# Source-number halves kept as 32-bit numbers in the attention loop's edge count

## The chip, the cores and the metric

The kernel is one program on one core of a Trainium2 chip. The metric is the time of one execution on the device, in microseconds (us); lower is better. Three runs before the change gave 5123.76 to 5125.2 us, median 5124.44 us.

## The reference, cut to what matters

A graph with 6250 nodes of 256 features and 200000 edges (`src`, `dst`, sorted by `dst`) goes through two blocks of graph layer and expert layer. The first graph layer is an attention over the edges:

```
h = einsum(layernorm(x), W)                # 8 heads of 32
e = leaky_relu(a_src[src] + a_dst[dst], 0.2)
e_exp = exp(e - segment_max(e, dst)[dst])
alpha = e_exp / (segment_sum(e_exp, dst)[dst] + 1e-16)
out = segment_sum(h[src] * alpha, dst)
```

The second graph layer scales each edge by the inverse roots of the two degrees of its ends, so it needs how often each node occurs in `src` and in `dst`:

```
in_deg  = segment_sum(w, src)
out_deg = segment_sum(w, dst)
```

The change lies in the counting of `src`.

## The kernel before

**Edge lists.** `edge_lists` reads the edges as 128 rows by 1792 numbers and splits each source number s into `hi` = s >> 7 (0 to 48) and `lo` = s - 128 hi (0 to 127). Both are written as bf16 tiles by the Vector engine (L691, L692) and stored by the SyncE queue in the DRAM tensor `source_halves` (L674; the places behind the last edge are filled from `src_void`, L670, L671).

**The attention loop.** `gat_edges` walks over 104 batches ("slots") of 16 tiles of 128 edges. A loop body holds four slots (RING = 4), so buffers rotate over four. Five engines work on different batches at one time, in an order written out by hand and kept by semaphores. In the slot in which the chain of batch k runs:

- GpSimd (POOL) issues 16 indirect DMAs a batch (L1262), each fetching 128 rows of 265 numbers by the source numbers in `gat_sources`. It runs up to three batches ahead.
- ScalarE (ACT) waits until all 16 gathers of batch k have landed, and packs their source terms (L1274).
- TensorE (PE) turns these terms (L1493), and sums earlier batches into PSUM (`scatter`, L1520), eight matrix products at a time between the small steps of the chain (L1497, L1504, L1506, L1510).
- The Vector engine (DVE) does, in this order: `count_onehots` of batch k-1 (L1344, two operations, `lo` then `hi`), then from the turned terms on the chain of batch k (L1353 to L1400), mixed with the messages (L1407) of batch k-1 and the adds of finished sums (L1430, L1429). The next slot begins with its `count_onehots`.

`count_onehots` waits for the batch's halves (`cl`) and for the products that read its outputs last (`sc`), writes two one-hots and signals `co`. The queue SP waits for `co` before it loads the halves of a later batch (L1231) and what stands behind that in its order: source numbers (L1235), flags (L1240, L1242), the transpose of the target one-hots (L1221), targets (L1246). TensorE multiplies the two one-hots (L1525) for the count, in step 3 of that batch, long after.

Of the kernel before, what the change touches and what calls it, by code (L numbers as in the profile page):

```python
# [13 lines left out]
BF16 = mybir.dt.bfloat16  # L14
# [5 lines left out]
P = 128  # L20
EPS = 1e-5
NEG_BIG = -1.0e38
CH = 16
# [7 lines left out]
BLK = 256  # L31
# [556 lines left out]
def edge_lists(k, S, ins, T, pj):  # L588

    nc = k.nc  # L590
    BG = S.BG
# [8 lines left out]
    with ExitStack() as ctx:  # L600
# [6 lines left out]
        df = k.sb(ctx, "dst_float", [P, BG, BLK])  # L607
        fs = k.sb(ctx, "starts_flag", [P, BG, BLK])
        fe = k.sb(ctx, "ends_flag", [P, BG, BLK])
        hi = k.sb(ctx, "src_hi", [P, BG * BLK], BF16)  # L610
        lo = k.sb(ctx, "src_lo", [P, BG * BLK], BF16)
        bulk, wrap = full * BLK, BLK // SPREAD
        assert bulk % CH == 0 and wrap % CH == 0 and (rest + 1) * SPREAD < P and bulk + wrap < S.BATCH * CH
        void = k.sb(ctx, "src_void", [P, 2, S.BATCH * CH - bulk], BF16)
        vd = k.sem("src_void_written")
        block = ctx.enter_context(nc.Block())
        src, dst = ins["src"], ins["dst"]
# [484 lines left out]
def gat_edges(k, S, C, T, acc):  # L1102
# [8 lines left out]
    RING = 4  # L1111
# [39 lines left out]
    with ExitStack() as ctx:  # L1151
# [23 lines left out]
        z = k.sb(ctx, "gat_sums", [P, 2 * TH + H])  # L1175
        q = k.sb(ctx, "gat_exponents", [P, TH + H])
        f = k.sb(ctx, "gat_factors", [1, 2, H])
        hl = k.sb(ctx, "count_halves", [P, RING, 2, CH], BF16)
        iob = k.sb(ctx, "count_iota", [P, P, 2], BF16)
        ohl = k.sb(ctx, "count_onehot_lo", [P, CH // 2, P, 2], BF16)  # L1180
        ohh = k.sb(ctx, "count_onehot_hi", [P, CH // 2, NT, 2], BF16)
# [1619 lines left out]
def gnn_moe_kernel(nc, ins, out):  # L2801
    S = Shapes(ins["x"], ins["src"], ins["L0_gnn_W"], ins["L0_ffn_W1"], ins["L1_ffn_w1"])
    NT, D, H = S.NT, S.D, S.H
    with ExitStack() as top:
        k = Core(nc, top)
        C, T = Namespace(), Namespace()
# [33 lines left out]
        T.flags = k.dram("gat_tile_flags", [S.SG * P * SUB, 2 * P])  # L2840
        T.least = k.dram("gat_tile_least", [2, S.SG * P * SUB])
        T.window = k.dram("gat_step_windows", [S.SG * P], I32)
        T.halves = k.dram("source_halves", [P, 2, S.BATCH * CH], BF16)
        T.steps = k.dram("unit_steps", [(S.SUPER + 1) * P, 2])
        T.codes = k.dram("unit_codes", [S.SUPER, P, 2 * P], BF16)
        T.xn = k.dram("normal_rows", [S.ROWS, D])
# [6 lines left out]
        with ExitStack() as gat:  # L2853
            C.adst = k.sb(gat, "a_dst_pieces", [P, NT, 3 * H], BF16)
            C.sources = k.sb(gat, "step_sources", [P, S.SG, P, SUB], I32)
            with ExitStack() as ctx:
                pj = Projection(k, S, C, T, ctx, x_res, ins["x"])
                setup(k, S, ins, C, pj)
                edge_lists(k, S, ins, T, pj)
                edge_tables(k, S, C, ins, T, pj)  # L2860
            k.recycle()
            gat_edges(k, S, C, T, acc)
# [67 lines left out]
```

## Time and profile before

| | |
|---|---|
| median of 3 runs | 5124.44 us |
| the profiled execution, its time | 5124.75 us |
| its span, first to last instruction | 5122.9 us |
| attention loop in the span | from 191 to 2355 us |
| Vector engine busy | 3459.0 us, 68% |
| GpSimd busy | 2300.1 us, 45% |
| TensorE busy | 4174.7 us, 81% |

The span is one execution seen by the hardware profiler; 1.85 us of the execution's own time lie outside it. A share of busy time is a mean over stages that have different limits: what matters for a change in the loop is which wait ends last in the loop.

### The profile page before, as it was taken

Reading aid. Unit: us, or ns where it says so; the run is one execution under the profiler, and the core shown is the slowest. Engines: PE = TensorE matmul, PEld = TensorE weight load, DVE = VectorE, ACT = ScalarE, POOL = GpSimd, SP = SyncE. Lnnn points to the kernel's source line nnn. Section 1 sums busy time; section 2 is a strip of 40 time slices with the busy share of each in tenths; the row PEclk is TensorE's granted clock in tenths of the full one; section 3 lists DMA queues with packets and bytes.
Section 4 is the critical chain, followed back from the end, with each engine's and each line's share of the span. In section 5 each row is a group of like instructions: output and inputs, shape, how many; then the busy total and the mean of one; then the engine's idle time right before and its main releaser. Section 6 shows DMA issues by size and latency. Waiting matters only on the chain. (4 is left out here: it accounts for less than half of the span.)

```text
span 5122.9 us, 87171 instructions
## 1 busy us (share of the span) xinstructions
PE 4174.7 (81%) x27202; PEld 3066.2 (60%) x27203; DVE 3459.0 (68%) x7696; ACT 1648.5 (32%) x2854; POOL 2300.1 (45%) x2330
## 2 busy tenths in 40 slices
PE   3477777777777777776699964799999999958998
PEld 2355555555555555555489953466666666557787
DVE  6366766676667667768622237899998999764444
ACT  1233333333333333333122236333333333231211
POOL 1377777777777777774155620000000000024553
PEclk9677777777777777776799986899999999958999
DMA  4766666666666666656167653454545545453432
GB/s 122 188 164 164 168 162 164 163 169 162 163 165 168 162 163 165 167 157 207 63 218 232 233 176 111 87 98 85 97 87 90 93 89 95 85 184 115 136 122 87
DMA packets 978900, 733.38 MB, mean 143 GB/s; under 512 B 735781, under 2 KB 864352, under 8 KB 976628
## 3 DMA queue, kind: packets, MB, share of 16 engines
q1 hardware_dynamic: 863047, 427.75, 32.6%
q0 software_dynamic: 109264, 296.24, 21.0%
q10 hardware_dynamic: 6364, 6.40, 0.4%
q8 instruction: 141, 2.31, 0.2%
q14 instruction: 84, 0.68, 0.0%
HBM read 485.07 MB, written 92.30 MB: 113 GB/s over the span
## 5 line engine op out<-in xcount | busy, mean ns | idle before, releaser
L1262 POOL DMA_INDIRECT gat_rows<-h_rows,gat_sources x1664 | 1621.9, 975 | 509.9 <-issue 478.8
L1520 PE MATMUL gat_sum_ps<-gat_rows,gat_onehot 128*128 128x265 f32 x3328 | 1261.7, 542 | 3.7 <-DVE gat_rows L1407 3.6
L1520 PEld LDWEIGHTS gat_sum_ps<-gat_rows,gat_onehot 128*128 128x128 f32 x3328 | 861.3, 272 | 218.2 <-DVE gat_rows L1407 4.8
L2207 ACT CAST gnn_z<-build_ps 128x392 bf16<-128x392 f32 x992 | 479.7, 485 | 749.4 <-PE build_ps L2222 749.2
L2231 PE MATMUL back_ps<-zb_pieces,gnn_z 128*128 128x384 bf16 x3038 | 634.6, 325 | 0.0
L2253 PE MATMUL front_ps<-x_res_wide,front_rows 128*128 128x448 bf16 x2604 | 618.1, 351 | 0.0
L2148 DVE TENSOR_TENSOR onehot_low<-dense_codes,dense_iota_bf 128x2048 bf16<-128x2048 bf16 x496 | 603.9, 1218 | 2.0 <-PE build_ps L2222 1.9
L2127 POOL DMA_INDIRECT front_rows<-zf_piece_rows,vrow_nodes x62 | 58.8, 948 | 1148.0 <-PE front_ps L2253 1137.9
L1407 DVE TENSOR_TENSOR gat_rows<-gat_rows,gat_numerators_ps 128x1024 f32<-128x1024 f32 x416 | 502.2, 1207 | 0.0
L2222 PEld LDWEIGHTS build_ps<-onehot_high,onehot_low 128*128 128x128 bf16 x7936 | 352.6, 98 | 184.9 <-issue 38.2
L2735 PE MATMUL moe_hidden_ps<-moe_rows_T,moe_w 128*128 128x256 f32 (+1 forms) x1408 | 450.4, 475 | 2.3 <-DMA moe_b<-in_L_ffn_b 1.5
L2761 ACT ACTIVATE moe_hidden<-moe_hidden_ps,moe_b 128x256 f32<-128x256 f32 (+1 forms) x352 | 194.0, 551 | 765.3 <-PE moe_hidden_ps L2735 765.3
L2745 PE MATMUL moe_out_ps<-moe_w,moe_hidden 128*128 128x256 f32 x1920 | 434.8, 384 | 1.1 <-ACT moe_hidden L2761 1.1
L2735 PEld LDWEIGHTS moe_hidden_ps<-moe_rows_T,moe_w 128*128 128x128 f32 x1408 | 377.5, 322 | 65.3 <-issue 4.8
L2222 PE MATMUL build_ps<-onehot_high,onehot_low 128*128 128x49 bf16 x7936 | 373.5, 188 | 44.0 <-DVE onehot_high L2148 41.5
L1430 DVE TENSOR_TENSOR x_res_wide<-x_res_wide,gat_sum_ps 128x265 f32 x832 | 355.7, 428 | 66.9 <-DVE x_res_wide L1430 66.4
L2745 PEld LDWEIGHTS moe_out_ps<-moe_w,moe_hidden 128*128 128x128 f32 x1920 | 360.1, 190 | 63.0 <-issue 13.9
L2231 PEld LDWEIGHTS back_ps<-zb_pieces,gnn_z 128*128 128x128 bf16 x3038 | 263.2, 97 | 150.7 <-issue 1.3
L1280 ACT ACTIVATE gat_numerators_ps<-gat_exponents 128x128 f32<-128x128 f32 x104 | 29.3, 281 | 906.2 <-DVE gat_exponents L1400 759.4
L2160 DVE TENSOR_TENSOR gnn_z<-gnn_z,front_ps 128x448 f32<-128x448 f32 x434 | 267.8, 617 | 74.8 <-PE front_ps L2253 73.3
L1493 PE MATMUL gat_turned_ps<-ident,gat_src_terms 128*128 128x128 f32 x104 | 49.3, 474 | 324.7 <-ACT gat_src_terms L1274 324.7
L2253 PEld LDWEIGHTS front_ps<-x_res_wide,front_rows 128*128 128x128 bf16 x2604 | 222.9, 97 | 139.8 <-issue 0.3
(377 smaller groups left out, 5467.5 us busy)
## 6 DMA issues: line engine op xcount, KB each, us to landing
moe_w<-in_L_ffn_W SPq DMA_DIRECT2D x112, 512.0 KB
gat_targets<-gat_step_targets SPq DMA_DIRECT2D x104, 512.0 KB
moe_w<-in_L_ffn_w SPq DMA_DIRECT2D x32, 1024.0 KB
gat_rows<-h_rows,gat_sources POOLq DMA_INDIRECT x1664
gat_flags<-gat_tile_flags SPq DMA_DIRECT2D x104, 128.0 KB
normal_rows<-moe_xn_all SPq DMA_DIRECT2D x14, 896.0 KB
mid_taken<-moe_rows_out SPq DMA_DIRECT2D x14, 896.0 KB, 7.4
moe_rows_out<-slot_zeros SPq DMA_DIRECT2D x24, 512.0 KB
```

The costliest lines, as they stand in the source:

```text
L1262: pool.indirect_dma_start(out=g[:, b, t, :], out_offset=None, in_=T.h[:, :], in_offset=bass.IndirectOffsetOnAxis(ap=idx[:, b, t:t + 1], ax ...
L1407: dve.tensor_tensor(rows[:, :, :, 0:HD], rows[:, :, :, 0:HD], pW[:, n * PART:(n + 1) * PART, :].unsqueeze(3).to_broadcast([P, PART, H, HD] ...
L1430: dve.tensor_tensor(window(w), window(w), po[:, s % BANKS, 0:W], ALU.add).then_inc(ad, 1)
L1520: last = pe.matmul(po[:, s % BANKS, 0:W], o[:, b, s * SUB + t, :], g[:, b, s * SUB + t, :], start=t == 0, stop=t == SUB - 1)
L2148: last = dve.tensor_tensor(out[:, n, :, :, :], ct[:, k % SLOTS, a, at].rearrange("p (u t) -> p u t", t=HITS).unsqueeze(2) .to_broadcast(sh ...
L2160: dve.tensor_tensor(yfT[:, at:at + CN], yfT[:, at:at + CN], pf[:, n, 0:CN], ALU.add).then_inc(ya, 1)
L2207: nc.scalar.copy(AT[:, k % 2, :, CHUNK * c:CHUNK * (c + 1)], pb[:, c % 2, 0:CHUNK * NT].rearrange("p (u h) -> p h u", u=CHUNK)).then_inc(a ...
L2222: last = pe.matmul(pb[:, c % 2, u * NT:(u + 1) * NT], ol[:, n, i, :, t], oj[:, n, i, :, t], start=True, stop=True)
L2231: ins = pe.matmul(py[:, (k - 1) % 2, 0:3 * P], AT[:, (k - 1) % 2, h, :], zb3[:, h, :, :].rearrange("p s f -> p (s f)"), start=h == 0, stop ...
L2253: ins = pe.matmul(pf[:, bank, 0:CN], zfv[:, first + s, m * P:(m + 1) * P], AV[:, first + s, chunk * CN:(chunk + 1) * CN], start=n == 0, st ...
L2735: last = pe.matmul(ph[:, f % 2, 0:tok], w1s[:, b, c, f:F:FC], xT[:, b, c, :], start=c == 0, stop=c == 1)
L2745: last = pe.matmul(py[:, q % 2, 0:D], hT[:, f, q * P:(q + 1) * P], w2s[:, b, f, :], start=f == 0, stop=f == FC - 1)
```

## The change

Five tensors (three tiles of the setup, one in DRAM, one tile of the loop) lose their bf16 type and take the default, 32-bit floating point: the tiles `src_hi`, `src_lo`, `src_void` of the setup, the DRAM tensor `source_halves`, and the loop's buffer `count_halves`. The one-hots and the row of numbers `count_iota` that the halves are compared with stay bf16. So both operations of L1344 now read one 32-bit and one bf16 operand and write bf16, and the stores and loads of the halves carry twice the bytes. No instruction is added, removed or moved.

```diff
@@ edge_lists
-        hi = k.sb(ctx, "src_hi", [P, BG * BLK], BF16)
-        lo = k.sb(ctx, "src_lo", [P, BG * BLK], BF16)
+        hi = k.sb(ctx, "src_hi", [P, BG * BLK])
+        lo = k.sb(ctx, "src_lo", [P, BG * BLK])
...
-        void = k.sb(ctx, "src_void", [P, 2, S.BATCH * CH - bulk], BF16)
+        void = k.sb(ctx, "src_void", [P, 2, S.BATCH * CH - bulk])
@@ gat_edges
-        hl = k.sb(ctx, "count_halves", [P, RING, 2, CH], BF16)
+        hl = k.sb(ctx, "count_halves", [P, RING, 2, CH])
         iob = k.sb(ctx, "count_iota", [P, P, 2], BF16)
@@ gnn_moe_kernel
-        T.halves = k.dram("source_halves", [P, 2, S.BATCH * CH], BF16)
+        T.halves = k.dram("source_halves", [P, 2, S.BATCH * CH])
```

## Rows read from the trace of the kernel before

**Rows 1.** Waits, stretch 400 to 2200 us: total, times, longest.
```profile
ACT gat_src_terms L1274 <- DMA gat_rows<-h_rows,gat_sources: 431.8, 88, 5.3
...
DVE gat_running L1353 <- PE gat_turned_ps L1493: 287.0, 88, 3.8
```

**Rows 2.** The page's groups: busy us, mean ns, idle before by releaser.
```profile
L1262 POOL DMA_INDIRECT gat_rows<-h_rows,gat_sources x1664 | 1621.9, 975 | 509.9 <-issue 478.8
```

**Rows 3.** By tile: duration ns min/median/max, first and last start.
```profile
L1344 DVE TENSOR_TENSOR count_onehot_lo<-count_halves,count_iota x104: 1224/1226/1227, 228.2 to 2342.7; 128x2048 bf16<-128x2048 bf16 x104
```

**Rows 4.** Timeline of one slot: start, duration, idle before in brackets.
```profile
1200.13 0.42 DVE L1353 TENSOR_TENSOR_SCAN gat_running<-gat_flags,gat_turned_ps 128x128 f32<-128x128 f32 x1 [3.23 <-PE gat_turned_ps L1493]
...
1207.28 0.17 DVE L1377 CUSTOM_DVE_ANT_0 gat_junk<-gat_small_ps,gat_tile_select 128x16 f32<-128x16 f32 x1 [1.43 <-PE gat_small_ps L1506]
...
1215.58 1.23 DVE L1344 TENSOR_TENSOR count_onehot_lo<-count_halves,count_iota 128x2048 bf16<-128x2048 bf16 x1 [0.51 <-PE gat_sum_ps L1520]
...
1216.37 1.25 POOL L1262 DMA_INDIRECT gat_rows<-h_rows,gat_sources  x1 [0.30 <-issue]
...
1216.72 0.56 DVE L1344 TENSOR_TENSOR count_onehot_hi<-count_halves,count_iota 128x784 bf16<-128x784 bf16 x1
...
1219.52 0.42 ACT L1274 COPY gat_src_terms<-gat_rows 128x128 f32<-128x128 f32 x1 [4.78 <-DMA gat_rows<-h_rows,gat_sources]
...
1220.51 0.42 DVE L1353 TENSOR_TENSOR_SCAN gat_running<-gat_flags,gat_turned_ps 128x128 f32<-128x128 f32 x1 [3.23 <-PE gat_turned_ps L1493]
```

**Rows 5.** Timeline, two more meetings of L1344 and a gather.
```profile
1257.07 1.23 DVE L1344 TENSOR_TENSOR count_onehot_lo<-count_halves,count_iota 128x2048 bf16<-128x2048 bf16 x1 [0.99 <-PE gat_sum_ps L1520]
1257.19 1.92 POOL L1262 DMA_INDIRECT gat_rows<-h_rows,gat_sources  x1 [0.30 <-issue]
...
1277.19 1.23 DVE L1344 TENSOR_TENSOR count_onehot_lo<-count_halves,count_iota 128x2048 bf16<-128x2048 bf16 x1 [0.43 <-PE gat_sum_ps L1520]
...
1278.26 0.97 POOL L1262 DMA_INDIRECT gat_rows<-h_rows,gat_sources  x1 [0.30 <-issue]
```

**Rows 6.** Timeline, indirect DMAs beside two other Vector operations.
```profile
102.96 0.97 DVE L1010 CUSTOM_DVE_ANT_0 gat_products<-gat_products 128x782 f32<-128x782 f32 x1
103.15 1.62 POOL L947 DMA_INDIRECT unit_steps<-part_steps,part_places  x1 [0.30 <-issue]
...
265.59 1.21 DVE L1407 TENSOR_TENSOR gat_rows<-gat_rows,gat_numerators_ps 128x1024 f32<-128x1024 f32 x1
265.66 0.95 POOL L1262 DMA_INDIRECT gat_rows<-h_rows,gat_sources  x1 [0.30 <-issue]
```

**Rows 7.** Timeline of the setup; by line in the loop: busy us, mean ns.
```profile
39.74 2.02 DVE L685 TENSOR_TENSOR starts_flag<-dst_int 128x1792 f32<-128x1792 int32 x1 [14.77 <-DMA dst_int<-in_dst]
...
L1407 DVE TENSOR_TENSOR gat_rows<-gat_rows,gat_numerators_ps 128x1024 f32<-128x1024 f32 x412 | 497.3, 1207 | 0.0
```

**Rows 8.** Timeline of products L1520: one slot, then the last chain's.
```profile
1199.89 3.81 PE L1520 MATMUL gat_sum_ps<-gat_rows,gat_onehot 128*128 128x265 f32 x8
...
1203.83 2.85 PE L1520 MATMUL gat_sum_ps<-gat_rows,gat_onehot 128*128 128x265 f32 x8
...
2328.38 0.42 DVE L1353 TENSOR_TENSOR_SCAN gat_running<-gat_flags,gat_turned_ps 128x128 f32<-128x128 f32 x1 [5.26 <-PE gat_turned_ps L1493]
...
2331.93 2.06 PE L1520 MATMUL gat_sum_ps<-gat_rows,gat_onehot 128*128 128x265 f32 x8
...
2334.59 0.17 DVE L1377 CUSTOM_DVE_ANT_0 gat_junk<-gat_small_ps,gat_tile_select 128x16 f32<-128x16 f32 x1 [0.52 <-PE gat_small_ps L1506]
```

**Rows 9.** Windows: length, busy and count by engine, PEclk, DMA, GB/s.
```profile
1201.00:1203.00 2.00, 2.00 (x6) 1.52 (x5) 1.78 (x5) 2.00 (x2) 1.40 (x2) 0.50 0.38 103
...
1205.60:1207.00 1.40, 1.40 (x9) 0.96 (x7) 0.24 (x1) 0.00 (x0) 1.09 (x2) 1.00 0.46 100
...
52.00:58.00 6.00, 0.00 (x0) 0.00 (x0) 6.00 (x9) 0.00 (x0) 0.00 (x0) 1.00 0.47 170
58.00:68.00 10.00, 0.00 (x0) 0.00 (x0) 9.56 (x52) 0.30 (x1) 0.00 (x0) 1.00 1.00 309
```

## The prediction

> **What bounds the loop now.** I read the waits of the loop first [rows 1]. ScalarE waits for the gathered rows 431.8 us in 88 slots of the stretch, and the Vector engine waits for TensorE's turn of those rows 287.0 us, 3.3 us a slot: its longest wait. So the Vector engine has slack in each slot, and what it waits for is the last of a batch's 16 gathers. Next the gathers themselves [rows 2]: GpSimd's idle time ahead of them is nearly all "issue", 0.30 us ahead of each, and it waits for no other engine to speak of. An undisturbed gather takes 0.945 us, 0.95 in [rows 6], and with the 0.30 that is 1.25 us a gather and 20.0 us for 16. But the mean gather takes 975 ns, so 104 batches lose (975 - 945) x 16 = 0.48 us each: 20.5, and the slot is 20.5 us: the counts start from 228.2 to 2342.7 us, 103 intervals of 20.53 [rows 3]. GpSimd is the bound, and what lengthens it is a few long gathers.
>
> **Where the 0.48 us is.** The timeline of one slot [rows 4] has a gather of 1.25 us, at 1216.37, during `count_onehot_lo` (1215.58 to 1216.81). Two more meetings [rows 5]: started 0.12 us after L1344, the gather takes 1.92; started 1.07 after it, 0.97. All three end 0.81 to 0.82 us after the end of the `lo` operation: 1216.81 + 0.81 = 1217.62; 1258.30 + 0.81 = 1259.11; 1278.42 + 0.81 = 1279.23. I read this as: a gather that starts while `lo` runs gets on only when `lo` has ended, between `lo` and `hi`, and ends 0.82 us later. These three stand for the meetings of the loop; the gather caught is always the sixteenth of its batch. Is it the kind of operation or its length? L1407, 1.21 us long, with one of its operands in PSUM, leaves a gather started 0.07 us after it at 0.95. L1010, which has both operands in SBUF and is 32-bit throughout, stretches one to 1.62, 0.84 us past its end [rows 6]. So two SBUF operands do it, 32-bit ones too.
>
> **The change, part by part.**
>
> *The two one-hots (L1344).* Now `lo` takes 1.226 us for 2048 elements [rows 3] and `hi` 0.56 for 784 [rows 4]: about 0.53 ns an element between them. Operations with 32-bit operands go at twice that: 1792 in 2.02 us with two SBUF operands, 1024 in 1.207 [rows 7], which makes 1.06 ns an element; 782 in 0.97 [rows 6]. One operand stays bf16, and the trace has no such mix. Bounds: 1.23 us if the pace is kept, 2.02 + 256 x 1.06 = 2.29 if it is lost; I take the upper one, 2.28, since every operation here with any 32-bit operand from SBUF is at that pace. So `lo` +1.055, `hi` 0.97 - 0.56 = +0.41.
>
> *What hides it on the Vector engine.* Both lie ahead of the 3.23 us wait at L1353 [rows 4]: +1.47 leaves 1.76 if the gathers did not move. Behind them on that engine stands only the chain, which waits anyway. The SP queue gets `co` 1.47 later and loads for a batch two further on than GpSimd's. Without the gathers, 103 of the 104 counts would cost nothing, and the last, with no gather behind it, +1.47 us.
>
> *What is late next.* The gather. It is caught by `lo`, so it ends 1.055 us later, and it is the one whose landing starts the next chain: it ends at 1217.62, ScalarE starts at 1219.52, the Vector engine's chain at 1220.51, so 2.89 us after it [rows 4]. From the chain's start (1200.13) to `lo` (1215.58) are 15.45 us that hold no count. `lo` and the caught gather then give 1.226 + 0.82 = 2.05, and 2.89 + 15.45 + 2.05 = 20.39, the slot of that timeline (20.38). The ring closes over the caught gather: `lo` lies on the path, `hi` does not, and what slack there is stays. Each slot grows by `lo`'s 1.055 us: 103 x 1.055 = 108.7.
>
> The rows thus show a gather held by an operation of the Vector engine that has two SBUF operands [rows 5, 6]. The Trainium skill ("SBUF — State Buffer", Who interferes with whom) is of two minds on this kind. It says that a Vector instruction with two SBUF inputs holds up a GpSimd instruction that reads SBUF; but also that a `tensor_tensor` was not seen to stall DMAs issued by GpSimd, since issuing them needs the write side (which it marks as inferred). By the second this term would be 0; by the rows it is 108.7, and the sum goes by the rows.
>
> *What shifts with it.* The piece from the chain's start to L1377 (7.15 us, [rows 4]) is TensorE's: sixteen products L1520, the first eight 3.81 us at a granted clock of 0.50, which is 1.2 GHz, the others 2.85, rising to 1.00, 2.4 GHz [rows 8, 9]. In the last chain, where the clock rose sooner, the second eight took 2.06 and the piece 6.21 us (2334.59 - 2328.38) [rows 8]. With all at 1.2 GHz the second eight would take 3.81 as well and the piece 8.1. A slot 1.05 us longer meets the changes of clock elsewhere; before, slots of the loop meet them nearly alike. Bounds -0.94 and +0.96 us a slot. I take -0.2, about one slot in five in the early form, because the extra time lies ahead of a chain that now begins low throughout, so a shift has more to win than to lose; this is a choice, the weakest term. 103 x -0.2 = -20.6.
>
> A slip in where the gathers stand against `lo` matters too: caught 0.05 us after its start, a gather loses 2.28 + 0.82 - 0.05 - 0.945 = 2.1 us; 1.25 after it, 0.9. Against 0.48 now that is +0.4 to +1.6 us a slot, +43 to +167 us in all, whatever the chain does.
>
> *Bytes.* The loop's loads of halves grow from 8 to 16 KB in as many pieces, for a batch that is counted slots later: nothing. In the setup the stores of `hi` and `lo` carry 0.79 MB more. They are issued as the DMA engines go into a stretch with a busy share of 0.47 (52 to 58 us), ahead of a full one, 309 GB/s [rows 9]. At that rate they need 2.5 us, and 6 x 0.53 = 3.2 are free: 0, bounds 0 and +2.5. The fill of `src_void` and the cast L691 keep their element counts and their pace to within 0.1 us.
>
> *Sum.* 5124.75 (the profiled execution's own time, 0.3 above the median) + 108.7 - 20.6 + 1.5 + 0 = 5214.3; less the 0.3: **5214 us**, 1.75% slower.
>
> **The rivals.**
>
> *Hidden.* The gathers are not held by the slower operation as they are by the fast one, and the Vector engine's wait takes it all: 5124.4 + 1.5 = 5126 us. It decides the sign, from the point where the caught gather's length no longer follows `lo`'s. For it: 3.23 us of slack. Against it: the 1.62 us beside a 32-bit operation [rows 6]. 6 in 100. The second of the Trainium skill's two statements above would lead here; the trace disagrees with it, with 1.92 us against 0.945.
>
> *Pace kept.* A bf16 output and one bf16 operand keep the pace: no change, 5124 us. No row of a mix speaks for it. 3 in 100.
>
> *Clock.* Each slot meets the early rise: -0.94 of the 1.055, so 103 x 0.115 + 1.5 = +13, 5138 us. All drift the other way: 103 x (1.055 + 0.96) + 1.5, 5333 us; it needs every slot at 1.2 GHz through the piece. 2 and 1 in 100.
>
> *Place.* The count starts so far from the sixteenth gather that the fifteenth or the next batch's first is caught, near 2 us each: about +160, 5285 us; from a count start over 1.25 us ahead of the sixteenth gather, where [rows 5] shows 1.07 already. As only some slots of the four in a body are so, some of this is in the forecast. 6 in 100. If instead the count moves behind the sixteenth gather, the chain is spared the hold and only the next batch pays; with early clocks that could end below 5114: 2 in 100.
>
> **How the numbers follow.** The forecast has 80 in 100, the rivals the rest. The range: rigid growth without the clock term is 5235 and with the setup's 2.5 and a little drift 5242; a clock term of -0.45 gives 5188. I take 5190 to 5242, which leaves out about 2 in 10. A measurement here tells 0.2% (10 us) from no change. Slower: 80 + 2 + 1 + 6 = 89, of which I give one to no change, so 0.88; within 0.2%: 6 + 3 + 1, so 0.10; faster 0.02.
>
> **What would show it.** In the changed kernel's profile: L1344 at about 2280 and 970 ns; the sixteenth gather of a batch at 2.0 to 3.0 us, ending 0.82 after `lo`; the mean gather at about 1040 ns; the wait at L1353 still near 3 us; the loop's counts 21.4 us apart; the rest of the kernel as before. Wrong would be: L1344 at the old pace; gathers at 0.95 beside it; or 1.8 us of wait at L1353 with slots of 20.5.

## The result, and the profile after

The changed kernel takes **5215.99 us** (median of 4 runs, 5215.21 to 5216.6) against 5124.82 (5123.76 to 5125.97) for the kernel before: a ratio of 1.0178, interval 1.016 to 1.0195. It is 91.2 us slower, where 5214 us were forecast.

First the page's head line of the changed kernel, and its group of gathers (busy us, mean ns, idle before by releaser), which answers to [rows 2].

```profile
span 5214.6 us, 87171 instructions
...
L1262 POOL DMA_INDIRECT gat_rows<-h_rows,gat_sources x1664 | 1712.3, 1029 | 510.0 <-issue 480.4
```

The gathers are busy 1712.3 us instead of 1621.9 and GpSimd's idle time before them is 510.0 instead of 509.9. So 90.4 of the 91.2 us lie inside the gathers.

The two operations of L1344, by tile (ns min/median/max, first and last start) as in [rows 3], and the second of them by line and form (busy us, mean ns, idle before):

```profile
L1344 DVE TENSOR_TENSOR count_onehot_lo<-count_halves,count_iota x104: 2291/2293/2337, 228.2 to 2433.5; 128x2048 bf16<-128x2048 f32 x104
```

```profile
L1344 DVE TENSOR_TENSOR count_onehot_hi<-count_halves,count_iota 128x784 bf16<-128x784 f32 x104 | 100.5, 967 | 0.0
```

`lo` went from 1226 to 2293 ns and `hi` from 0.56 us to 967 ns. The counts start from 228.2 to 2433.5 us, 103 intervals of 21.41 us instead of 20.53: 0.88 a slot. The last count starts 90.8 us later than it did [rows 3]. From there to the end of the span it is 2781.1 us, and it was 2780.2.

Waits of 400 to 2200 us (total, times, longest), against [rows 1]:

```profile
ACT gat_src_terms L1274 <- DMA gat_rows<-h_rows,gat_sources: 527.2, 84, 7.1
...
DVE gat_running L1353 <- PE gat_turned_ps L1493: 264.1, 84, 4.2
```

The Vector engine got 1.47 us more of work a slot (1.067 + 0.41) in a slot that is 0.88 longer, so 0.59 us comes out of its waits. At L1353 it still waits 264.1 / 84 = 3.14 us, only 0.12 less than before; most of the rest comes from the wait at L1377, shown further down. It still has over 3 us of slack, and the loop is slower all the same. ScalarE waits 6.3 us a slot for the gathered rows, which was 4.9.

Two slots of the timeline (start, duration, idle before in brackets) answer to [rows 4, 5]:

```profile
1130.73 0.95 POOL L1262 DMA_INDIRECT gat_rows<-h_rows,gat_sources  x1 [0.30 <-issue]
1130.74 2.31 DVE L1344 TENSOR_TENSOR count_onehot_lo<-count_halves,count_iota 128x2048 bf16<-128x2048 f32 x1 [0.99 <-PE gat_sum_ps L1520]
1131.99 1.89 POOL L1262 DMA_INDIRECT gat_rows<-h_rows,gat_sources  x1 [0.30 <-issue]
1132.98 0.96 DVE L1344 TENSOR_TENSOR count_onehot_hi<-count_halves,count_iota 128x784 bf16<-128x784 f32 x1
...
1135.78 0.42 ACT L1274 COPY gat_src_terms<-gat_rows 128x128 f32<-128x128 f32 x1 [6.36 <-DMA gat_rows<-h_rows,gat_sources]
...
1151.18 2.29 DVE L1344 TENSOR_TENSOR count_onehot_lo<-count_halves,count_iota 128x2048 bf16<-128x2048 f32 x1 [0.43 <-issue]
1151.72 2.56 POOL L1262 DMA_INDIRECT gat_rows<-h_rows,gat_sources  x1 [0.30 <-issue]
1153.39 0.97 DVE L1344 TENSOR_TENSOR count_onehot_hi<-count_halves,count_iota 128x784 bf16<-128x784 f32 x1
1154.59 0.95 POOL L1262 DMA_INDIRECT gat_rows<-h_rows,gat_sources  x1 [0.30 <-issue]
```

A gather that starts after `lo` has started ends 0.8 us after `lo` ends: 1130.74 + 2.31 = 1133.05, and the gather ends at 1133.88; 1151.18 + 2.29 = 1153.47, and the gather ends at 1154.28. The gather of 1154.59 follows the second one, so the held one is the fifteenth of its batch there. In 23 of the 90 slots of batches 10 to 99 `lo` holds the fifteenth, in the other 67 the sixteenth. In the kernel before, the gather that met `lo` was the sixteenth in all 90, and it was lengthened by more than 0.05 us in 71 of them. The gather of 1130.73 started 0.01 us ahead of `lo` and was not held.

### The profile page after: what moved, and what is told of

Same layout as the page of the kernel before. It is cut to its first block and busy times, and to the rows that moved or that the text cites. A ratio compares the mean times of both kernels' runs of the same rounds, so it can differ in the third digit from the quotient of the medians.

```text
span 5214.6 us, 87171 instructions
## 1 busy us (share of the span) xinstructions
PE 4151.2 (80%) x27202; PEld 3027.2 (58%) x27203; DVE 3611.6 (69%) x7696; ACT 1650.0 (32%) x2854; POOL 2390.3 (46%) x2330
## 3 DMA queue, kind: packets, MB, share of 16 engines
q8 instruction: 141, 2.31, 0.2%
## 5 line engine op out<-in xcount | busy, mean ns | idle before, releaser
L1262 POOL DMA_INDIRECT gat_rows<-h_rows,gat_sources x1664 | 1712.3, 1029 | 510.0 <-issue 480.4
L1520 PE MATMUL gat_sum_ps<-gat_rows,gat_onehot 128*128 128x265 f32 x3328 | 1180.7, 514 | 1.7 <-DVE gat_rows L1407 1.5
L1520 PEld LDWEIGHTS gat_sum_ps<-gat_rows,gat_onehot 128*128 128x128 f32 x3328 | 796.3, 251 | 189.7 <-DVE gat_rows L1407 2.4
L2693 POOL DMA_INDIRECT moe_rows<-normal_rows,moe_slot_source x176 | 169.5, 963 | 289.0 <-POOLq L2450 234.0
```

Source lines behind the costliest of these rows:

```text
L1262: pool.indirect_dma_start(out=g[:, b, t, :], out_offset=None, in_=T.h[:, :], in_offset=bass.IndirectOffsetOnAxis(ap=idx[:, b, t:t + 1], ax ...
L1520: last = pe.matmul(po[:, s % BANKS, 0:W], o[:, b, s * SUB + t, :], g[:, b, s * SUB + t, :], start=t == 0, stop=t == SUB - 1)
```

## The experiments

Each was compared with runs of the kernel before on the same chip, which took 5127.7 us beside e1 to e4, 5128.3 beside e5, e7, e8 and e9, and 5128.0 beside e6, e10, e11 and e12. Ratios are against these, with their intervals.

### One half at a time: e1_lo_wide and e2_hi_wide

```diff
-        hl = k.sb(ctx, "count_halves", [P, RING, 2, CH], BF16)
+        hl = [k.sb(ctx, f"count_halves_{a}", [P, RING, CH], w) for a, w in enumerate((BF16, F32))]
...
-                sp.dma_start(hl[:, b, :, :], T.halves[:, :, bass.ds(n * CH, CH)]).then_inc(cl[b], 16)
+                for h in range(2):
+                    sp.dma_start(hl[h][:, b, :], T.halves[h][:, bass.ds(n * CH, CH)]).then_inc(cl[b], 16)
```

The other kernel has `(F32, BF16)`. The DRAM tensor and the setup's buffers are split in the same way, so both have one more load a batch.

> Only the lo half is kept in 32 bits (its own DRAM tensor and buffer, so one more small load a slot); the hi half stays bf16. Theory (a gather is held until the lo operation ends, hi lies in slack): the whole growth of the change, 5215 us, within 5; lo at 2.29 us, hi at 0.56, the held gathers end 0.82 us after lo, counts 21.3 to 21.4 us apart. Rival (the Vector engine's busy time is what counts): 1.06 of 1.47 us a slot, so 72% of the growth, 5190 us. Rival (bytes of the halves): half the growth, 5170 us.

> Only the hi half is kept in 32 bits. Theory: hi grows from 0.56 to 0.98 us and costs nothing, since a held gather gets on between the two operations and the Vector engine has over 3 us of slack at L1353: 5125 us, within 3, held gathers as long as before (1.2 to 1.9 us). Rival (busy time counts): 28% of the growth, 5150 us. Rival (bytes): 5170 us.

Measured: `lo` alone 5218.66 us, 1.0176 (1.0159 to 1.0193); `hi` alone 5130.53, 1.0004 (0.9994 to 1.0013). Each kernel's gathers, from its page:

```profile
L1265 POOL DMA_INDIRECT gat_rows<-h_rows,gat_sources x1664 | 1711.7, 1029 | 510.4 <-issue 481.6 <-PE gat_sum_ps L1523 25.3 <-DMA gat_sources<-step_sources 3.6
```

```profile
L1265 POOL DMA_INDIRECT gat_rows<-h_rows,gat_sources x1664 | 1623.9, 976 | 510.4 <-issue 480.0 <-PE gat_sum_ps L1523 26.8 <-DMA gat_sources<-step_sources 3.5
```

The whole loss comes with `lo`. The `hi` operation grew to 968 ns in the second kernel as well and cost nothing: the wait behind it, the same one as L1353, gave it back. Over 400 to 2200 us it went from 287.0 to 250.7 us, which is 88 x 0.41.

### The bytes: e3_bytes

```diff
-        hl = k.sb(ctx, "count_halves", [P, RING, 2, CH], BF16)
+        hl = k.sb(ctx, "count_halves", [P, RING, 2, 2 * CH], BF16)
...
-                sp.dma_start(hl[:, b, :, :], T.halves[:, :, bass.ds(n * CH, CH)]).then_inc(cl[b], 16)
+                sp.dma_start(hl[:, b, :, :], T.halves[:, :, bass.ds(n * CH, 2 * CH)]).then_inc(cl[b], 16)
```

> The kernel before, with halves in bf16, but each load of halves fetches twice the elements (16 KB a slot in place of 8, the second half of them unused). Theory: no change, 5125 us within 3. Rival (the doubled loads delay what stands behind them): up to the whole growth, 5216 us.

Measured: 5128.19 us, 1.000 (0.9991 to 1.001), gathers at 975 ns. The loop's larger loads cost nothing that can be measured here.

### One-hots against PSUM: e4_psum_after and e6_psum_before

The row of numbers that the halves are compared with goes into a free part of the PSUM bank of `gat_numerators_ps`. The first is the changed kernel with this, the second the kernel before, with 16-bit halves; in both the row is 32-bit. The count now also waits for the numerators of its batch, which share the bank (the last line).

```diff
-        iob = k.sb(ctx, "count_iota", [P, P, 2], BF16)
...
-        pW = k.ps(ctx, "gat_numerators_ps", [P, TILES, H])
+        pWI = k.ps(ctx, "gat_numerators_ps", [P, 512])
+        pW = pWI[:, 0:TILES * H].rearrange("p (t h) -> p t h", h=H)
+        iob = pWI[:, TILES * H:TILES * H + 2 * P].rearrange("p (w t) -> p w t", t=2)
...
+                dve.wait_ge(ex, j + 1)
```

> The changed kernel with the row of numbers that the halves are compared with in PSUM (32-bit, in the free part of the bank of gat_numerators_ps) in place of SBUF, and a wait of the count for the numerators before it, which are written 0.8 us earlier anyway. The two operations then have one SBUF operand. Theory (two SBUF operands hold the gather): they stay at 2.2 to 2.4 and 0.9 to 1.1 us, yet no gather is held, each takes 0.95 us beside them; GpSimd issues 16 gathers in 20.0 to 20.1 us, and the loop runs at that: 5080 us, within 8, so faster than both kernels. Rival (a long Vector operation beside a gather costs, wherever it reads): 5216 us. Rival (no hold, but the Vector engine's longer work comes onto the path): about 5125 us.

> The kernel before with bf16 halves, and the row of numbers that they are compared with in PSUM in 32 bits. Theory: the operations lose the pace as in the changed kernel, with 2.29 and 0.97 us, and hold no gather; the same as the changed kernel with the row in PSUM, 5092 us within 5. So it is the place of the second operand that decides and not the width of the halves. Rival (the width of the halves matters by itself): another time than 5092 us by 10 us or more.

Measured: 5091.75 us, 0.9928 (0.9911 to 0.9944), and 5086.63 us, 0.9924 (0.9908 to 0.9941). Both beat both kernels. The first is 3.8 us above the range that was expected (5080 within 8), the second 0.4 us below its own (5092 within 5), far from the 10 us of its rival. In the first, by tile, timeline and page:

```profile
L1346 DVE TENSOR_TENSOR count_onehot_lo<-count_halves,gat_numerators_ps x104: 2286/2287/2289, 230.3 to 2306.5; 128x2048 bf16<-128x2048 f32 x104
```

```profile
1218.42 2.29 DVE L1346 TENSOR_TENSOR count_onehot_lo<-count_halves,gat_numerators_ps 128x2048 bf16<-128x2048 f32 x1 [0.50 <-issue]
...
1218.91 0.95 POOL L1263 DMA_INDIRECT gat_rows<-h_rows,gat_sources  x1 [0.30 <-issue]
...
1220.16 0.94 POOL L1263 DMA_INDIRECT gat_rows<-h_rows,gat_sources  x1 [0.30 <-issue]
```

```profile
L1263 POOL DMA_INDIRECT gat_rows<-h_rows,gat_sources x1664 | 1582.2, 951 | 510.2 <-issue 485.5 <-PE gat_sum_ps L1522 21.3 <-DMA gat_sources<-step_sources 3.4
```

`lo` is as slow as in the changed kernel (2287 against 2293 ns), and two gathers start during it and take 0.95 and 0.94 us. So the length of `lo` is not what costs: it is the gather held during it, and it is held when both operands come from SBUF. Counted over the batches 10 to 99 of the first kernel, 161 gathers start during `lo` and 73 during `hi`, and none of them takes over 1.0 us.

In the tile row of the second kernel the 16-bit halves are not faster there:

```profile
L1346 DVE TENSOR_TENSOR count_onehot_lo<-count_halves,gat_numerators_ps x104: 2286/2289/2290, 227.1 to 2298.3; 128x2048 bf16<-128x2048 bf16 x104
```

The gain was 36 us where 45 were expected: the counts of the first are (2306.5 - 230.3) / 103 = 20.16 us apart, and not 20.0 to 20.1. About 0.1 us a slot is left in small holds. In the first kernel 42 of the 1440 gathers of batches 10 to 99 take over 1.0 us, up to 1.14. Each started during a short operation of the chain that also reads two SBUF operands (L1385, L1393, L1397 or L1401), for example:

```profile
673.34 0.43 DVE L1397 SCALAR_TENSOR_TENSOR gat_sums<-gat_sums 128x264 f32<-128x264 f32 x1
673.53 1.07 POOL L1263 DMA_INDIRECT gat_rows<-h_rows,gat_sources  x1 [0.31 <-issue]
```

This one too ends 0.83 us after the operation that it met. The 612 gathers of these batches that start during L1409, L1420 or L1432, which read one operand from PSUM and one from SBUF, take at most 0.96 us.

### `lo` cut in two: e5_split_after and e7_split_before

```diff
-                    shape = [P, CH // 2, w, 2]
-                    last = dve.tensor_tensor(out[:, :, :, :],
-                                             hl[:, b, half, :].rearrange("p (u t) -> p u t", t=2).unsqueeze(2).to_broadcast(shape),
-                                             iob[:, 0:w, :].unsqueeze(1).to_broadcast(shape), ALU.is_equal)
+                    parts = 2 if half else 1
+                    per = CH // 2 // parts
+                    shape = [P, per, w, 2]
+                    pairs = hl[:, b, half, :].rearrange("p (u t) -> p u t", t=2)
+                    for m in range(parts):
+                        at = slice(m * per, (m + 1) * per)
+                        last = dve.tensor_tensor(out[:, at, :, :], pairs[:, at, :].unsqueeze(2).to_broadcast(shape),
+                                                 iob[:, 0:w, :].unsqueeze(1).to_broadcast(shape), ALU.is_equal)
```

> The changed kernel (32-bit halves), with the lo operation cut in two of 1024 elements, 1.22 us each; nothing else. The Vector engine does the same elements with one fixed cost more. Theory (a gather is held only until the operation under way ends): most of the growth goes, though the Vector engine works longer than in the changed kernel; slots of 20.6 us, 5138 us (5130 to 5150). Rival (Vector engine busy time): 5230 us. Rival (a gather waits until the Vector engine has no two-operand work in its queue): 5220 us or more.

> The kernel before (bf16), with the lo operation cut in two of 1024 elements, 0.68 us each. Theory: the hold gets shorter, slots of 20.27 us against 20.48, 5105 us (5095 to 5115). Rival (busy time): 5125 to 5140 us.

Measured: the cut in the changed kernel 5218.15 us, 1.0177 (1.016 to 1.0194), as slow as uncut, where 5138 was expected. That is near the 5220 of the second rival, that a gather waits until the Vector engine has no two-operand work left. The cut in the kernel before 5101.29 us, 0.9948 (0.9932 to 0.9965): 27 us gained, in the range expected (5095 to 5115). The timeline of the first decides against the rival and shows what the expectation left out:

```profile
1024.44 2.36 DVE L1349 TENSOR_TENSOR count_onehot_lo<-count_halves,count_iota 128x1024 bf16<-128x1024 f32 x2 [0.43 <-PE gat_sum_ps L1524]
1025.31 1.18 POOL L1262 DMA_INDIRECT gat_rows<-h_rows,gat_sources  x1 [0.30 <-issue]
1026.72 0.97 DVE L1349 TENSOR_TENSOR count_onehot_hi<-count_halves,count_iota 128x784 bf16<-128x784 f32 x1
1026.79 1.71 POOL L1262 DMA_INDIRECT gat_rows<-h_rows,gat_sources  x1 [0.30 <-issue]
```

The first gather ends at 1026.49, while `lo` goes on until 1026.80: it was let go between the two pieces (1.18 us). But the next one comes 1.48 us later, 0.07 us into `hi`, and is held to its end: 1.71. What the cut spares one gather, the following operation takes from the next. The whole count lasts 3.3 us here, which is more than the 2.5 us of two undisturbed gathers; cut in the kernel before, it lasts 1.8.

### The order of the two: e10_hi_first

```diff
-                for out, half, w in ((ohl, 1, P), (ohh, 0, NT)):
+                for out, half, w in ((ohh, 0, NT), (ohl, 1, P)):
```

> The changed kernel with the order of the two operations reversed: hi (0.97 us) and then lo (2.29). The sixteenth gather, which starts the chain, is then held by hi alone, and the first gather of the next batch by lo. Theory as the runs so far bear it out (GpSimd's issue is a queue that is always full, so any gather held costs the slot): 1.2 to 1.5 us held a slot, 5210 to 5235 us. Rival (only the gather that starts the chain counts, as the prediction's ring had it): the chain gets off 1.3 us sooner, 5110 to 5130 us.

Measured: 5233.99 us, 1.0205 (1.0188 to 1.0222), in the range that the theory gave, and slower than the changed kernel: its counts are 21.56 us apart, 0.15 more. Its timeline:

```profile
750.14 0.98 DVE L1344 TENSOR_TENSOR count_onehot_hi<-count_halves,count_iota 128x784 bf16<-128x784 f32 x1 [0.51 <-issue]
750.61 1.32 POOL L1262 DMA_INDIRECT gat_rows<-h_rows,gat_sources  x1 [0.30 <-issue]
751.04 2.28 DVE L1344 TENSOR_TENSOR count_onehot_lo<-count_halves,count_iota 128x2048 bf16<-128x2048 f32 x1
752.24 1.90 POOL L1262 DMA_INDIRECT gat_rows<-h_rows,gat_sources  x1 [0.31 <-issue]
```

Each of the two operations holds a gather here, `hi` the fifteenth and `lo` the sixteenth. That is so in 39 of the 90 slots. In 27 others `lo` holds the fifteenth or the sixteenth, and `hi` none or the fourteenth. In the last 24 `lo` holds the first gather of the next batch, in 19 of them with the sixteenth held by `hi`. The sixteenth then ends 1.38 us before the end of `lo`, where in the changed kernel it ends at least 0.82 after, and so the chain that hangs on it is spared `lo`. These 24 slots, from one sixteenth gather's end to the next, take 20.26 us on average, but the slot after each takes 22.55, because its batch begins with the held gather: 21.4 us for the two together. A held gather need not be the one that the chain waits for: whichever it is, it moves all that stand behind it in GpSimd's queue.

### TensorE's clock: e11_clock_before and e12_clock_after, e8_warm_before and e9_warm_after

Extra products, which nobody reads, ahead of TensorE's wait for the turned rows: 5 in one pair of kernels, 12 in the other, each pair once on the kernel before and once on the changed one.

```diff
-                pe.wait_ge(us, k + 1)
                 until(pe, mx, k)
                 until(pe, eq, k)
+                for _ in range(5):
+                    pe.matmul(pXM[:, :, :], C.ident[:, :], C.ident[:, :].unsqueeze(1).to_broadcast([P, 2, P]), start=True, stop=True)
+                pe.wait_ge(us, k + 1)
```

> The kernel before, with 12 matrix products of 128 x 256 added to TensorE's gap ahead of each chain (into a PSUM tile that is overwritten next, results unused), to hold its granted clock at 1.00 through the loop. It makes the piece of the chain from L1353 to L1377 6.0 us long in place of 7.1. By itself no gain is expected, since the count then starts earlier against the gathers and holds the fifteenth: slots of 20.6 us, 5139 us (5120 to 5150). It is the base for the next kernel. Rival (the chain alone sets the slot): 20.0 us, 5080 us.

> The changed kernel with the same 12 products in the gap. Theory (the growth of the change is the lo operation's 1.06 us a slot or a little more, and the clock's shift took 0.2 of it back): with the clock held, the growth against the run before with these products is 1.06 to 1.15 us a slot, 109 to 118 us, so about 5255 us. Rival (the clock has no part, and the smaller growth of 0.88 us has another cause): growth of 91 us again.

> The kernel before with 5 in place of 12 products of 128 x 256 in TensorE's gap: the 12 took 7.1 us a slot and made TensorE the bound, at 0.30 us for each of their 24 parts; 5 should take 3.0 us, about the gap. Slots of 20.5 to 20.7 us, 5125 to 5145 us, with the chain's piece from L1353 to L1377 at 6.0 to 6.3 us in place of 7.1. Base for the next.

> The changed kernel with the same 5 products. Theory (growth is the hold by the lo operation, 1.06 us a slot, and the shift against the clock's changes took 0.2 of it back in the change): growth against the run before with 5 products of 1.0 to 1.15 us a slot, 103 to 118 us: 5230 to 5260 us. Rival (the clock has no part in the size of the growth): 91 us.

With 12: 5457.64 us, 1.0643 (1.0625 to 1.0661), and 5455.39 us, 1.0635 (1.0617 to 1.0653). Both expectations were missed (5139, and 5255 with a growth of 109 to 118 us). The 24 parts in which the trace shows the 12 products take 7.14 us (first row, timeline of the first kernel), and TensorE became the bound, as the two pages show: GpSimd now waits for it 299.0 and 196.1 us, and its idle time ahead of a slot's 16 gathers, 4.9 us in the kernel before (509.9 / 104), is 7.7 and 6.8.

```profile
1204.14 7.14 PE L1493 MATMUL gat_turned_ps<-ident 128*128 128x256 f32 x24
```

```profile
L1262 POOL DMA_INDIRECT gat_rows<-h_rows,gat_sources x1664 | 1632.6, 981 | 802.7 <-issue 500.3 <-PE gat_sum_ps L1522 299.0 <-DMA gat_sources<-step_sources 3.4
```

```profile
L1262 POOL DMA_INDIRECT gat_rows<-h_rows,gat_sources x1664 | 1741.1, 1046 | 707.0 <-issue 507.5 <-PE gat_sum_ps L1522 196.1 <-DMA gat_sources<-step_sources 3.4
```

They serve for something else. From the first to the second the gathers grew by 108.5 us, GpSimd's wait for TensorE shrank by 102.9, and the median did not grow (-2.3 us, though the profiled execution of the second, 5470.89 us, is the longest of its runs and 13 us above that of the first). With GpSimd no longer the bound, the change costs nothing that stands out from the scatter of these runs.

With 5: 5130.91 us, 1.0005 (0.9995 to 1.0014), and 5237.39 us, 1.0217 (1.02 to 1.0234). The windows of 400 to 2200 us (busy and count by engine; then the granted clock, DMA share, GB/s), one kernel each: before, changed, before with 5 products, changed with 5.

```profile
400.00:2200.00 1800.00, 1399.89 (x6776) 1008.12 (x6776) 1256.47 (x3256) 595.22 (x616) 1371.70 (x1407) 0.76 0.61 165
```

```profile
400.00:2200.00 1800.00, 1322.40 (x6520) 933.30 (x6518) 1330.95 (x3123) 568.70 (x591) 1388.76 (x1351) 0.76 0.60 159
```

```profile
400.00:2200.00 1800.00, 1430.53 (x7629) 1052.26 (x7628) 1252.70 (x3245) 594.62 (x613) 1372.54 (x1403) 0.88 0.63 164
```

```profile
400.00:2200.00 1800.00, 1404.83 (x7291) 1022.64 (x7289) 1317.36 (x3094) 565.31 (x587) 1392.14 (x1339) 0.87 0.59 157
```

The mean granted clock rose from 0.76 to 0.88 and 0.87, and the change costs 106.5 us there by the medians, instead of 91.2. That lies in the 103 to 118 that the clock's part of the theory gave, at its lower end; between the counts of the two profiled executions it is 102.3 us, 0.99 a slot.

## Why the prediction was right, step by step

**The two one-hots: right.** 2.28 and 0.97 us were taken for a mix of widths that no row showed; 2.293 and 0.967 were measured. Between its two bounds, 1.23 and 2.29 us, the prediction had chosen the right one.

**Who pays: right, and shown.** A gather is held until `lo` ends and then ends 0.8 us later. Shown by taking away what holds it: with the second operand in PSUM and `lo` as slow, the mean gather is 951 ns and the kernel is 36 us faster than before the change. In the kernels `before`, `after` and the two with a PSUM operand, every gather of batches 10 to 99 that takes over 1.0 us starts during an operation with two SBUF operands. The rows went against the Trainium skill ("SBUF — State Buffer", Who interferes with whom) where it says that a `tensor_tensor` was not seen to stall DMAs issued by GpSimd. The runs bear the rows out: 1.89 and 2.56 us beside two SBUF operands, 0.95 beside one.

**`hi` and the bytes: right.** Both cost nothing (1.0004 and 1.000). The setup, bound 0 to 2.5 us: the counts begin at 228.2 us in both kernels. The last count, forecast +1.5: the stretch from its start to the end of the span grew by 0.9.

**"The ring closes over the caught gather": it holds as a sum here, but the condition that it put on the cost is too narrow.** The prediction added up a slot from the sixteenth gather's end to the next one's. The means of these pieces over the slots of batches 10 to 99, worked out from the timelines, all in us:

| kernel | slot | gather's end to chain | chain to L1377 | chain to `lo` | `lo` | end of `lo` to gather's end |
|---|---|---|---|---|---|---|
| before | 20.48 | 2.92 | 7.09 | 15.52 | 1.23 | 0.82 |
| changed | 21.33 | 2.90 | 6.57 | 15.00 | 2.29 | 1.14 |
| e11_clock_before | 20.54 | 3.86 | 6.07 | 14.50 | 1.23 | 0.96 |
| e12_clock_after | 21.52 | 2.99 | 6.16 | 14.58 | 2.29 | 1.66 |

(The slot is the sum of the third, the fifth and the last two.) The other count is GpSimd's own. The interval of the counts (tile rows) less 16 mean gathers (pages):

| kernel | interval, us | mean gather, ns | interval - 16 gathers | 16 x (mean - 945), us |
|---|---|---|---|---|
| before | 20.53 | 975 | 4.93 | 0.48 |
| changed | 21.41 | 1029 | 4.95 | 1.34 |
| e4_psum_after | 20.16 | 951 | 4.94 | 0.10 |
| e6_psum_before | 20.11 | 948 | 4.94 | 0.05 |
| e7_split_before | 20.29 | 959 | 4.95 | 0.22 |
| e10_hi_first | 21.56 | 1038 | 4.95 | 1.49 |
| e11_clock_before | 20.59 | 978 | 4.94 | 0.53 |
| e12_clock_after | 21.58 | 1040 | 4.94 | 1.52 |

The 4.94 are nearly all the 16 x 0.306 us between gathers (509.9 / 1664). So in these kernels the slot is 16 gathers with no pause beyond that, and the last column is all that the Vector engine adds. Of the 0.48 in the kernel before, 0.42 lie in gathers that start during `lo`; the rest are the small holds beside short operations of the chain, which the prediction did not mention. The prediction read GpSimd's queue as the bound at its start, but then worked out the cost by the first count, in which the held gather is the one that starts the chain. With `hi` first that is no longer so in 24 of the 90 slots, and the cost stays. The second count is the wider one: with it the gain of the kernels with a PSUM operand can be read off as well, 0.38 and 0.43 us a slot.

**The clock's -0.2 us, and what is missing from the sum: two terms, both mis-sized, that cancel.** By the first table the growth of 0.85 us a slot (0.88 over all 103) is

- +1.07 for `lo` (forecast +1.055);
- -0.52 for the piece up to L1377 (forecast -0.2, with bounds of -0.94 and +0.96), and the whole way to `lo` shortened by the same 0.52. The piece is under 6.5 us in 47 of the 90 slots and was so in none before; the forecast had one slot in five;
- +0.32 after `lo` (forecast 0). In the 67 slots in which the sixteenth is held it ends 0.82 us after `lo`, as forecast. In 23 slots it is the fifteenth, the sixteenth then follows it, and ends 2.07 after `lo`: 23 x 1.25 / 90 = 0.32;
- -0.02 for the gather's end to the chain.

That the total came within 2 us of the forecast is therefore luck. Each of the two terms was off by 0.32 us a slot, 33 us in all, and with either error alone the time would have been 5183 or 5249 us, outside the range of 5190 to 5242.

The forecast's text had the +0.32 as the rival *Place*, and as something partly in the forecast. It and the -0.52 belong together: where the chain is short, `lo` comes early (14.33 us after the chain's start in those 23 slots, 15.23 in the 67), and meets the fifteenth gather.

That the short piece is TensorE's shows in the two rows below, waits of 400 to 2200 us and one slot's timeline. The wait at L1377 is 73.0 / 84 = 0.87 us a slot. In the kernel before, the same stretch has 121.1 us in 88 slots, 1.38. The second eight products of this slot take 2.14 us against 2.85 [rows 8].

```profile
DVE gat_junk L1377 <- PE gat_small_ps L1506: 73.0, 84, 1.5
```

```profile
1204.60 2.14 PE L1520 MATMUL gat_sum_ps<-gat_rows,gat_onehot 128*128 128x265 f32 x8
...
1207.34 0.17 DVE L1377 CUSTOM_DVE_ANT_0 gat_junk<-gat_small_ps,gat_tile_select 128x16 f32<-128x16 f32 x1 [0.72 <-PE gat_small_ps L1506]
```

The pair with 5 products tests this, though not cleanly. There the piece has its short form in both kernels (6.07 and 6.16 us), the -0.52 is gone, and the change costs more: 0.98 us a slot by the first table. But two other pieces move as well: the gather's end to the chain by -0.87 us and the end of `lo` to the gather's end by +0.70. In the other count, the gathers that start during `lo` or `hi` grow by 0.83 us a slot from the kernel before to the changed one, and by 1.01 in this pair. So the size of the growth depends on where the gathers meet `lo`, and it comes near to `lo`'s own 1.07 where the piece is short in both kernels. That the clock alone makes the difference is not shown. Why the clock rises sooner in the changed kernel (the mean of the stretch is 0.76 in both) was argued from the longer slot and not shown either.

**The rivals.** *Hidden* fell with the changed kernel's own rows: the held gathers grew with `lo`, up to 2.56 us in the rows above, and over 3 us of wait at L1353 hid none of it. *Pace kept* fell with the 2.293. *Clock* in its full size did not happen: -0.52 and not -0.94. *Place* happened in one slot of four, as above, and not in all.

## What to carry to other kernels

Slack of an engine says what its own growth costs, not what its operations do to others; look at how long the bounding engine's instructions take while the operation runs, and compare them with the undisturbed ones. Where a queue never pauses, as here, the slot is the sum of its instructions, and every stretched one is paid in full, whichever the chain hangs on. Where another engine is the bound, as with the 12 extra products, the same stretch cost nothing measurable. Here the remedy was not a faster operation (16-bit, 1226 ns) but one that does not hold the queue (an operand in PSUM, 2287 ns): 36 to 41 us under the kernel before.

## What the hardware did that was not expected

- Cutting the holding operation in two lets the gather through at the cut. That gains when the pieces are short (0.69 us each: mean gather 975 to 959 ns) and nothing when they are long (1.2 us: 1029 to 1028 ns), since the next gather is caught by the next operation. A start 0.07 us into an operation is enough (1026.79 against 1026.72, 1.71 us); a start 0.01 us ahead of one is free (1130.73, 0.95 us).
- The pace of an operation with two 16-bit operands (1226 ns for 2048 elements) is lost in full when one of them is 32-bit: 2293 ns with 32-bit halves. It took 2289 ns with 16-bit halves and the 32-bit row in PSUM, where no run separates the width from the place. The Trainium skill ("VectorE: DVE Perf Modes", The perf-mode tier table) has 1224 ns for a bf16 and 2293 ns for a 32-bit `tensor_tensor` of 2048 elements in SBUF; this case's traces agree with both, and the mixed pair has the slower one.
- Short operations with two SBUF operands hold gathers as well, by up to 0.2 us (0.43 us long: 1.07 us in place of 0.945). These holds are what is left of the Vector engine's part in the kernels with a PSUM operand.
- Five extra products a slot on TensorE, in a gap, raised its mean granted clock in the loop from 0.76 to 0.88 at no cost in time (1.0005), and at no gain either.
